# Four chained graph networks on one core: the first attention product of gathered, own and late node rows in the fetching stage, x loaded once, marks of slots as bytes

## The reference

```python
x = _layernorm(x + SAGE(x, src, dst))        # three layers, 128 -> 256 -> 256 -> 128
x = _layernorm(x + GAT(x, edge_index))       # two attention layers, a graph norm after each, a mean over edges
x = _layernorm(x + JK(x, src, dst))          # four layers, maximum over the layers, a linear layer
x = _layernorm(x + GCN(x, edge_index))       # three layers
# SAGE layer:  relu(h @ Ws + (segment_sum(h[src], dst) / deg) @ Wn + b)
# GAT layer:   h = x @ W;  e = leaky_relu((h*att_src)[src] + (h*att_dst)[dst])
#              alpha = softmax of e over the edges of a destination, its own loop included
#              out = segment_sum(h[src] * alpha, dst) + b
```

## Time and profile before

| | |
|---|---|
| time, median of 3 runs | 6671.77 us (6668.97 to 6678.84) |
| the profiled execution's own time | 6708.78 us |
| span of its instructions | 6707.0 us |
| TensorE busy in the span | 71% |
| VectorE | 67% |
| ScalarE | 46% |
| POOL | 60% |
| DMA moved | 1292.14 MB, mean 193 GB/s |

### The profile page before, as it was taken

How to read it: one execution, slowest core, us unless ns; L and a number is a source line. 1 busy time by engine, 2 the same in 40 slices (tenths; PEclk the granted TensorE clock), 3 DMA queues, 4 the chain that set the end, 5 groups by cost and what they waited for, 6 DMA issues and landing times. The chain is left out here.

```text
span 6707.0 us, 86620 instructions
## 1 busy us (share of the span) xinstructions
PE 4759.6 (71%) x23528; PEld 3219.0 (48%) x23532; DVE 4488.5 (67%) x13695; ACT 3059.6 (46%) x6979; POOL 4001.4 (60%) x3991
## 2 busy tenths in 40 slices
PE   6899998989988724796335445445999996598221
PEld 4667776645568403694223222222666664465111
DVE  4788887333369827788885566676888886654554
ACT  3556665643334104453444333434777773355000
POOL 5566664754445477667667666575333335674777
PEclk9999999989999755795557776756999998899555
DMA  6999886987779424795446798865777775676332
GB/s 152 232 263 277 255 254 208 288 242 245 241 226 267 125 54 109 240 347 157 126 132 151 126 135 125 138 94 139 263 268 268 268 252 183 202 213 175 90 95 82
DMA packets 1104141, 1292.14 MB, mean 193 GB/s; under 512 B 133903, under 2 KB 815679, under 8 KB 1097390
## 3 DMA queue, kind: packets, MB, share of 16 engines
q1 hardware_dynamic: 973518, 1032.63, 49.6%
q0 software_dynamic: 130144, 253.97, 20.1%
HBM read 607.93 MB, written 682.10 MB: 192 GB/s over the span
## 5 line engine op out<-in xcount | busy, mean ns | idle before, releaser
L570 POOL DMA_INDIRECT jk_layer_msg<-jk,idx_jk x588 | 592.3, 1007 | 278.0 <-issue 174.0
L1057 PE MATMUL jk_layer_sum_ps<-ident,jk_layer_weighted 128*128 128x128 f32 x784 | 184.0, 378 | 562.9 <-ACT jk_layer_weighted L1023 562.9
L2090 POOL TENSOR_TENSOR rows_x_b<-rows_x,w_gcn_b 128x512 f32<-128x512 f32 x98 | 125.7, 1283 | 581.2 <-DVE rows_y L2214 581.2
L1057 PEld LDWEIGHTS jk_layer_sum_ps<-ident,jk_layer_weighted 128*128 128x128 f32 x784 | 117.7, 187 | 682.7 <-ACT jk_layer_weighted L1023 682.7
L696 PE MATMUL sage_nodes_h_ps<-sage_nodes_h_t,w_ws 128*128 128x512 f32 x784 | 353.4, 593 | 0.0
L1198 DVE COPY sage_h<-sage_turn 128x512 f32<-128x512 f32 x98 | 67.8, 692 | 420.9 <-PE sage_turn L687 420.9
L2284 PE MATMUL gcn_end_sum_ps<-ident,gcn_end_rows 128*128 128x128 f32 x196 | 54.7, 434 | 384.6 <-DVE gcn_end_rows L2277 384.6
L894 ACT ACTIVATE sage_nodes_h_t<-sage_nodes_h_ps,w_b_c 128x512 f32<-128x512 f32 x392 | 248.1, 684 | 168.3 <-PE sage_nodes_h_ps L696 168.3
L570 POOL DMA_INDIRECT sage_msg<-h,idx x196 | 185.2, 945 | 231.7 <-ACT sage_weighted L1023 152.2
L1886 ACT ACTIVATE jk_layer_h_t<-jk_layer_h_ps,w_jk_b 128x512 f32<-128x512 f32 x196 | 134.7, 687 | 402.6 <-PE jk_layer_h_ps L696 338.8
L696 PE MATMUL jk_layer_h_ps<-jk_layer_sum_t,w_jk_w 128*128 128x512 f32 x392 | 312.4, 893 | 0.6 <-DVE jk_layer_sum_t L1079 0.4
(11 more groups left out here) (454 smaller groups left out, 16082.4 us busy)
## 6 DMA issues: line engine op xcount, KB each, us to landing
h<-sage_nodes_h SPq DMA_DIRECT2D x196, 512.0 KB
h_t<-sage_h_t SPq DMA_DIRECT2D x98, 512.0 KB
h<-sage_h SPq DMA_DIRECT2D x98, 512.0 KB, 3.5
jk_t<-jk_layer_h_t SPq DMA_DIRECT2D x196, 256.0 KB
rows_layers<-jk_t SPq DMA_DIRECT2D x49, 1024.0 KB, 4.8
r<-rows_h SPq DMA_DIRECT2D x98, 512.0 KB, 2.8
second_x_in<-u SPq DMA_DIRECT2D x147, 260.0 KB
jk<-jk_layer_h SPq DMA_DIRECT2D x147, 256.0 KB, 4.5
```

What stands on the lines that cost most here:

```text
L570: pool.indirect_dma_start(out=into[:, g.number % depth, s, :], out_offset=None, in_=table, in_offset=bass.IndirectOffsetOnAxis(ap=index_ti ...
L1057: mm = pe.transpose(ps[:, c, at_s], self.weighted[:, g.b, s, c * P:(c + 1) * P], self.K.ident[:])
L2090: pool.tensor_tensor(x3_b[:, g.number % deep], x3[:, g.b], to_subs(W.row["gcn2_b"]), ALU.add).then_inc(x3_biased.sem, 1)
```

## The change

- The node stage loads x once, into seven buffers, and keeps it until the residual sum has read it. It stores the first norm of every node group to a table x1. It makes u only for the first 49 node groups (`EARLY`).
- The set-up stage writes the marks of slots as bytes to a table `goes`; the node stage loads them in seven broadcasts, in place of 49 loads of destinations and 49 comparisons.
- `sage_end_block` stores x1 alone; u and its scores are no longer made there.
- `fetch_block` becomes `first_product_block`: for each slot group it works three items, the rows of x1 that the sources name (gathered), the slots' own rows (loaded), and a late node group (loaded). Each is turned, copied, multiplied and put out with the bias: to `kept`, to u and `K.att`, to u and `node_stats`. The source counts run beside them, with four mark buffers in place of two.
- u has rows of 128 columns, not 130; the attention blocks' tiles are narrowed to match.

```diff
@@ setup_block
+        dve.tensor_copy(goes_r[:, 1:RJ], K.cont[:, 1:RJ])
+        dve.tensor_copy(goes_r[:, 0:1], link_f[:]).then_inc(goes_ready, 1)
...
-        sp.wait_ge(edges_in, 16 * edge_loads)
...
+        sp.wait_ge(goes_ready, 1)
+        sp.dma_start(tables["goes"].rearrange("(q j) -> q j", j=RJ), goes_r[:]).then_inc(goes_stored, 16)
@@ SourceCounts (buffers t % 2 become t % 4)
-        wait_for(dve, self.hot_used, Group(t - 2))
+        wait_for(dve, self.hot_used, Group(t - 4))
@@ sage_nodes_block
         def load(g):
-            wait_for(sp, turned, g.lag(2))
+            wait_for(sp, y_summed, g.lag(x_deep))
...
-        def reload(g):
-            wait_for(sp, y_summed, g.lag(2))
...
         def store_u(g):
-            wait_for(sp, u_biased, g)
-            sp.dma_start(at(node_rows(tables["u"], SLOTS), g), u[:, g.b]).then_inc(u_stored.of(g), 16)
-        def load_near(g):
-            if g.number < EG:
-                wait_for(sp, near_used, g.lag(2))
-                sp.dma_start(near[:, g.b, :], tables["dst"][cols(g, GROUP, 0, GROUP + 2)].partition_broadcast(P)).then_inc(near_in.of(g), 16)
+            if g.number < EARLY:
+                wait_for(sp, u_biased, g)
+                sp.dma_start(at(node_rows(tables["u"], SLOTS), g), u[:, g.b]).then_inc(u_stored.of(g), 16)
+        def store_x1(g):
+            wait_for(sp, norm.done, g)
+            sp.dma_start(at(node_rows(tables["x1"], SLOTS), g), z[:, g.b]).then_inc(z_stored.of(g), 16)
+        def load_goes(g):
+            if g.number % GOES_EVERY == GOES_EVERY // 2:
+                part = slice(g.number // GOES_EVERY * GOES_PART, (g.number // GOES_EVERY + 1) * GOES_PART)
+                sp.dma_start(K.goes_on[:, part], tables["goes"][part].partition_broadcast(P)).then_inc(goes_in, 16)
...
-        stages = [(load, -1), (load_near, 6), (reload, 3), (store_h1, 3), (store_h2, 4), (store_u, 7), (store_y, 6)]
+        stages = [(load, -1), (load_goes, 6), (store_h1, 3), (store_h2, 4), (store_x1, 5), (store_u, 7), (store_y, 6)]
...
         def turn_x1(g):
+            if g.number >= EARLY:
+                return
...
         def make_u(g):
+            if g.number >= EARLY:
+                return
...
-            layer_rows(pe, ring[:, :, 0:D + 2], [(W.wide["gat1"][:, :, 0:D + 2], x1_t[:, g.b])]).then_inc(u_made.sem, 1)
+            layer_rows(pe, ring[:, :, 0:D], [(W.m["gat1"], x1_t[:, g.b])]).then_inc(u_made.sem, 1)
...
         def apply(g):
             wait_for(dve, x1_turned, g.lag(2))
+            wait_for(dve, z_stored, g.lag(2))
             norm.vector_apply(dve, g, y, z)
...
-        def masks(g):
...
-        stages = [(residual, 4), (apply, 5), (second, 5), (apply2, 6), (count_u, 6), (masks, 7)]
+        stages = [(residual, 4), (apply, 5), (second, 5), (apply2, 6), (count_u, 6)]
@@ sage_end_block
-        run_groups(pe, EG, [(lambda g: sums.tensor_sum(pe, g), 0), (make_u, 3), (make, 1), (turn_x1, 2)])
+        run_groups(pe, EG, [(lambda g: sums.tensor_sum(pe, g), 0), (make, 1)])
...
-        run_groups(dve, EG, [(lambda g: sums.vector_carry(dve, g, [made]), 0), (out_att, 3), (apply, 2), (add, 1)])
+        run_groups(dve, EG, [(lambda g: sums.vector_carry(dve, g, [made]), 0), (apply, 2), (add, 1)])
@@ first_product_block, in place of fetch_block
+    EDGE, SLOT, LATE = 0, 1, 2
+    n_items = 3 * EG
...
+    def counts_of(i):
+        r, k = turn_of(i)
+        return range(4 * r, 4 * r + 2) if k == EDGE else range(4 * r + k + 1, 4 * r + k + 2)
...
+        def load(i):
...
+            wait_for(sp, turned, item_of_load(n.lag(3)))
+            source = at(slot_rows(tables["x1"]), Group(r)) if k == SLOT else at(node_rows(tables["x1"], SLOTS), Group(EARLY + r))
+            sp.dma_start(x_in[:, n.number % 3], source).then_inc(loaded.of(n), 16)
...
+        run_groups(sp, n_items, [(load, -5), (store, 3)])
+        counts.sync_store(sp)
...
+    @block.gpsimd
+    def _(pool):
+        for r in range(EG):
+            g = Group(r)
+            if r >= 4:
+                wait_for(pool, turned, Group(3 * (r - 4)))
+            for s in range(SUB):
+                pool.indirect_dma_start(out=msg[:, r % 4, s, :], out_offset=None, in_=tables["x1"],
+                                        in_offset=bass.IndirectOffsetOnAxis(ap=K.idx[:, cols(g, SUB, s, 1)], axis=0)).then_inc(fetched.of(g), 16)
+    @block.tensor
+    def _(pe):
+        def turn(i):
...
+            wait_for(pe, copied, i.lag(2))
+            turn_rows(pe, x_ps[i.b], rows, K.ident).then_inc(turned.sem, 1)
+        def make(i):
+            r, k = turn_of(i)
+            wait_for(pe, copied, i)
+            if k == EDGE:
+                wait_for(pe, edge_out, Group(r - 1))
+                out, w = wide_ps[0][:, :, 0:D + 2], W.wide["gat1"][:, :, 0:D + 2]
...
+            layer_rows(pe, out, [(w, x_t[:, i.b])]).then_inc(made.sem, 1)
...
+        run_groups(pe, n_items, [(turn, 0), (make, 1), (count_sources, 2)])
...
+        run_groups(act, n_items, [(copy, 0), (scores, 2)])
...
+        def out(i):
...
+            wait_for(dve, made, i)
+            if k == LATE:
...
+                dve.tensor_tensor(node_u[:, g.b], lanes(node_ps, D), to_subs(W.row["gat1_b"]), ALU.add).then_inc(node_out.sem, 1)
+                wait_for(dve, node_out, g)
+                for s in range(SUB):
+                    ins = dve.bn_stats(tables["node_stats"][:, cols(Group(EARLY + r), SUB, s, 1), :], node_u[:, g.b, s, :])
...
+            for half in range(2):
...
+                ins = dve.tensor_tensor(rows, wide_ps[k][:, subs, 0:width], bias[:, 0:width].unsqueeze(1).broadcast_to([P, 2, width]), ALU.add)
...
+        run_groups(dve, n_items, [(mark_sources, 0), (out, 1)])
+        counts.vector_keep(dve)
```

More of the change, by code:

```diff
@@ L571, in pool_gather @@
                                 in_offset=bass.IndirectOffsetOnAxis(ap=index_tile[:, cols(g, SUB, s, 1)], axis=0)).then_inc(arrived.of(g), 16)
[L574 to L603, removed]
 def places_block(nc, K, tables):
@@ L826, in _ @@
         last = Group(NG - 1)
-        wait_for(pool, turned, last.lag(2))
-        pool.memset(x_in[:, last.b], 0.0).then_inc(pads_zero, 1)
-        wait_for(pool, y_summed, last.lag(2))
-        pool.memset(x_again[:, last.b], 0.0).then_inc(pads_zero, 1)
+        wait_for(pool, y_summed, last.lag(x_deep))
+        pool.memset(x_in[:, last.number % x_deep], 0.0).then_inc(pads_zero, 1)
     @block.tensor
@@ L923, in out_u @@
             for half in range(2):
-                ins = act.copy(u[:, g.b, 2 * half:2 * half + 2, :], ring[:, 2 * half:2 * half + 2, 0:D + 2])
+                ins = act.copy(u[:, g.b, 2 * half:2 * half + 2, :], ring[:, 2 * half:2 * half + 2, 0:D])
             ins.then_inc(u_out.sem, 1)
@@ L1406, in attend_block @@
     S, A_ = ph.count_sem, ph.dma_sems
-    heads, rows_wide = (2, D + 2) if first else (1, D)
+    heads = 2 if first else 1
     m = D // heads
     table = tables["u"] if first else tables["yv"]
-    own = ph.sb("own", [P, 3, SUB, rows_wide])
+    own = ph.sb("own", [P, 3, SUB, D])
     own_scaled, weighted = ph.sb("own_scaled", [P, 2, SUB, D]), ph.sb("weighted", [P, 2, SUB, D])
-    rows, sum_t = ph.sb("rows", [P, 3, SUB, rows_wide]), ph.sb("sum_t", [P, 2, GROUP])
+    rows, sum_t = ph.sb("rows", [P, 3, SUB, D]), ph.sb("sum_t", [P, 2, GROUP])
     sum_ps, g_ps = ([ph.ps(f"{k}{b}", [P, GROUP]) for b in range(2)] for k in ("sum_ps", "g_ps"))
@@ L1469, in _ @@
     def _(dve):
-        if first:
-            dve.memset(rows[:, :, :, D:rows_wide], 0.0)
         dve.memset(sum_t[:, 1, GROUP - 1:GROUP], 0.0).then_inc(zeroed, 1)
@@ L2491, in resnorm_gnn @@
     both = SLOTS + NODES_PAD
-    tables = {"dst": dram("dst_pad", SLOTS + 16, 0, I32), "place": dram("place", NODES_PAD, 1, I32), "counts": dram("counts", NODES_PAD, 1)}
-    for name, width in (("h1", HID), ("h2", HID), ("x2", D), ("x3", D), ("r1", HID), ("y2", D)):
+    tables = {"goes": dram("goes", SLOTS, 0, U8), "place": dram("place", NODES_PAD, 1, I32), "counts": dram("counts", NODES_PAD, 1)}
+    for name, width in (("h1", HID), ("h2", HID), ("x1", D), ("x2", D), ("x3", D), ("r1", HID), ("y2", D)):
         tables[name] = dram(name, both, width)
-    tables["u"], tables["yv"] = dram("u", SLOTS + both, D + 2), dram("yv", SLOTS + both, D)
+    tables["u"], tables["yv"] = dram("u", SLOTS + both, D), dram("yv", SLOTS + both, D)
     tables["jk_t"] = nc.dram_tensor("jk_t", [EG, P, LAYERS, GROUP], F32, kind="Internal").ap()
```

220 lines of the change are left out of this document (140 added, 80 removed).

## The result

The kernel after takes 6551.06 us (median of 4 runs, 6543.28 to 6553.56), the kernel before in the same comparison 6670.37 (6668.66 to 6678.84): ratio 0.982, 95% interval 0.9809 to 0.9832, 119 us less. The forecast was 6541 with 6490 to 6608. The profiled execution took 6543.28 us around a span of 6541.5.

The account below looks back on a forecast made before the run. Node stage bound by DMA early, TensorE later; last layer by VectorE; fetching stage by POOL alone. Terms -42 - 54 - 8 - 36 + 9 = -131 us gave 6541 us from a median of 6671.77, range 6490 to 6608.

Parts of the forecast that it names:

- Node stage, DMA-bound half (-42): Early node stage, 26 groups: fewer bytes moved per group save 42 us, with ends 0 and -55.
- At the rate of this stretch that is 12.55 x 2560/2821 = 11.39 us: Early node stage: a group falls from 12.55 us in proportion to its KB, saving 1.16 x 26 = 30 us.
- A sign of being wrong: Early node stage: DMA still at 1.00 and 12.5 us a group would show the forecast wrong.
- TensorE-bound half and end (-54, -8): Later node stage: no x1 turn or u product saves 54 us; shorter u chain at the end, net 8 us.
- POOL, the near competitor: Later node stage: POOL needs 9.1 us a group, level with TensorE's 9.12, so it might hold the pace.
- The stall at the last load: Node stage end: TensorE's 6.91 us wait for the last x load, behind POOL's last memset, stays.
- Last message layer (-36): Last message layer: VectorE loses score copy and bias, 32 us, and the block's end some 4: -36 us.
- Fetching stage (+9): New stage replacing the fetching stage: three engines close together, 274 us against 265, +9; ends -6 and +63.
- I take 5.3: New stage: 5.3 us for each of 49 rounds, with TensorE, VectorE and POOL close together.
- 1 (the node stage gives little back): Node stage: first half keeps its pace, POOL holds the other at 9.8 us; -51 in all, 6621 us; chance 0.12.
- 2 (half clock): New stage runs at half clock, 10.1 us a round, +244; kernel slower at 6776 us; chance 0.05.
- 3 (a gather waits out a mark): New stage: port contention makes each gather 1.74 us, +90 in place of +9; kernel 6622 us; chance 0.06.

Follow-up runs that it names:

- the marks' part alone: Kernel before with only the slot marks changed, to seven byte loads for 49 broadcasts and comparisons: 6665.84 us against 6688.62, ratio 0.9972.
- the second series of the kernel after: Kernel after unchanged, five runs on the same chip as the version with the padding zeroed earlier: 6555.67 us, ratio to the kernel before 0.9811.
- the second profile: Kernel before profiled again with no edit: span 6692.6 us, its series median 6688.62; groups 4 to 49 took 515.5 us.

## Why the prediction was right, and which step was not

The trace of the kernel before had a stretch that bears on the first step below: with ten of the broadcasts still issued in it, the same stage moved 280 GB/s with TensorE hardly idle.

```profile
500.00:600.00 100.00, 99.70 (x581) 71.97 (x579) 85.56 (x330) 62.74 (x133) 69.00 (x67) 1.00 1.03 280
```

- **Node stage, DMA-bound half (-42).** The step that failed: "At the rate of this stretch that is 12.55 x 2560/2821 = 11.39 us". It took the rate for fixed, and the bytes for the cause. The stretch above already spoke against that. Shown by the runs: with as many bytes as before DMA ran at 273 GB/s and TensorE was idle for 3.5 of 201 us, and without 40 small writes the start ran at TensorE's pace. A sign of being wrong came half true: DMA stood at 1.00 until 240 us, and groups 5 to 8 took 12.3 to 13.8 us. Measured: groups 4 to 49 from 525.8 and 515.5 us to 480.6 to 492.4 in seven profiles, about -33; by the times of the marks' part alone, 10 to 27 us. The number was half a guess between 0 and -55, and it was too high. Why the broadcast of 257 KB cost more here than a second load of x of 256 KB (516 to 526 us with the one, 496 with the other, in which the store of u is 4 KB smaller and VectorE makes no comparisons) is open.
- **TensorE-bound half and end (-54, -8).** Right, in the mechanism and the size: 524.9 and 525.9 us from group 49 to the stage's end became 460.5 and 461.4, -64 for -62. POOL, the near competitor, kept up: TensorE has no idle time in the 400 us shown. The stall at the last load stayed, as said, and was 8.24 us where it had been 6.91.
- **Last message layer (-36).** Right: 365.7 to 325.7 us, -40; putting the slots back gives 363.7.
- **Fetching stage (+9).** The mechanism (three engines close together) was right, the size not: the step "I take 5.3" was 5.05, since the marks slow a gather by 14 ns instead of the 0.1 us of the earlier trace rows that the sum kept, and VectorE and TensorE fit under POOL's pace. Measured -2.
- **Sum.** By the profiles -33 - 64 - 40 - 2 = -139 for -131, by the medians -119 (and -125 beside the second series of the kernel after). The last three terms differ by some 2 us at most between profiles. If they hold in the other executions too, the medians leave -13 to -19 for the first half of the node stage, which agrees with the 10 to 27 us of the marks alone: by this account -42 was 23 to 29 us too much and the other terms together 17 too little, -106 for -89. That the time came out within 10 us of the forecast is then partly luck, two errors that offset each other. The term -42 was also read from an execution 38 us above the median, in which that half was 10 us longer than in the second profile. Why the profiles give -33 there and the times less is not settled.
- **Rivals.** 1 (the node stage gives little back) fell with 9.13 us a group; 2 (half clock) with a granted clock of 1.00; 3 (a gather waits out a mark) with 1.249 us without marks and 1.263 with them.

Left open: a version that keeps all writes of places but starts them some twenty steps later wasn't run, so what the writes would cost there is not known.

## What to carry to other kernels

A DMA share near 1.0 is no limit in bytes by itself (here 193 to 291 GB/s at shares of 0.95 to 1.03): before a stretch is priced by its bytes, look for one that moves more bytes per us, in the same kernel first, and test the smallest writes as well as the largest. Work moved into a stage that another engine's list sets can cost next to nothing up to the pace of the second engine (under 3 us here for a third of the items); two runs, one that thins the setter and one that thins the rest, tell how far that is. Behind an in-order list, look for a small job at its end that somebody waits for: here one memset moved 20 us forward gave back 11.

## What was not expected of the hardware

Leaving out 40 scattered writes of 128 slot numbers each, two a group beside 2560 KB of other traffic, took the mean packet of another queue, in one execution, from 0.151 and 0.168 us to 0.108 and the start of the stage from 103 to 115 us down to 94. The middle packet is the same; what goes are the few that take over 500 ns, some 450 to 490 of them in 125 us against 33. In the steady part of the stage, with DMA at 0.84 to 0.94, the same writes stand beside hardly a stretched group, though long packets are there too (317 in 120 us). Why the start alone suffers is not shown. The Trainium skill, DMA: Bandwidth & Descriptors, section Why small descriptors are slow (HBM only), gives each packet a fixed cost besides its bytes. No run here measures that cost by itself; what the runs show is a delay in the packets of the other queue.
